# Experts' constants: summed on VectorE and added to X inside the expert slots instead of after them

## What is computed

```python
logits = xf @ wr + br
topk_vals, topk_idx = jax.lax.top_k(logits, K)            # K = 2 of E = 4
gates = jax.nn.softmax(topk_vals, axis=-1)
h = gelu(jnp.einsum('nd,edh->enh', xf, w1) + b1[:, None, :])
y = jnp.einsum('enh,ehd->end', h, w2) + b2[:, None, :]
c = jnp.einsum('eh,ehd->ed', gelu(b1), w2) + b2           # what expert e gives for a zero row
c_sum = c.sum(axis=0)
out = einsum('nk,nkd->nd', gates, y_sel - c_sel + c_sum)  # y_sel, c_sel: rows of the chosen experts
```

## Time and profile before

| | |
|---|---|
| median of 3 runs | 2856.28 us (2854.46 to 2858.55) |
| the profiled execution's own time | 2849.76 us |
| its span, first to last instruction | 2847.9 us |
| mean granted TensorE clock | 0.957 of full speed |
| TensorE busy | 2592.6 us (91%) |
| VectorE busy | 1286.4 us (45%) |
| GpSimd busy | 841.2 us (30%) |
| ScalarE busy | 691.1 us (24%) |

### The profile page before, as it was taken

One profiled execution on the slowest core, in us unless ns is written; L12 is line 12 of the kernel. 1 busy time (PEld: TensorE's weight loads), 2 busy tenths in 40 slices (PEclk: granted clock), 3 DMA queues, 4 the chain that ended last, 5 costly groups with the idle time before them and its releaser, 6 DMA issues.

```text
span 2847.9 us, 29154 instructions
## 1 busy us (share of the span) xinstructions
PE 2592.6 (91%) x10019; PEld 1794.1 (63%) x10019; DVE 1286.4 (45%) x2138; ACT 691.1 (24%) x1127; POOL 841.2 (30%) x794
## 2 busy tenths in 40 slices
PE   5996888978999959999999999999999997966987
PEld 3552333434444448888888888887777676845776
DVE  8785666441111273010010010017888887856554
ACT  2001222121111123121121121124444443123232
POOL 1225665001111055555300000105454451004443
PEclk9998999988999979999999999999999998987999
DMA  4016666163333244232222222226777785447864
GB/s 140 1 38 186 183 180 170 60 227 128 109 118 111 73 156 178 78 107 79 79 100 87 77 80 104 92 77 217 237 230 251 260 250 192 136 177 268 293 236 143
DMA packets 170693, 420.59 MB, mean 148 GB/s; under 512 B 26857, under 2 KB 27657, under 8 KB 170593
## 3 DMA queue, kind: packets, MB, share of 16 engines
q0 software_dynamic: 63008, 191.21, 21.7%
q1 hardware_dynamic: 80320, 178.20, 17.9%
q10 hardware_dynamic: 27264, 49.88, 4.7%
HBM read 332.76 MB, written 92.57 MB: 149 GB/s over the span
## 4 chain that ended last, share of the span: by engine, by line
PE 80%; DVE 7%; DMA 5%; issue 4%; ACT 1%; another core or an unknown queue 1%; POOL 1%; DVEq 1%; SPq 0%; ACTq 0%; POOLq 0%
PE pair L1096 10%; PE pair L1095 10%; PE pair L1094 10%; PE pair L1017 6%; PE pair L1037 6%; PE pair L937 5%; PE pair L879 3%; PE pair L955 2%; PE pair L1118 2%; PE pair L1138 2%; PE pair L1139 2%; PE pair L1140 2%; PE pair L1121 2%; PE pair L919 2%; PE pair L901 2%
## 5 line engine op out<-in xcount | busy, mean ns | idle before, releaser
L1094 PE MATMUL pair<-wh,xh 128*128 128x512 f32 x1200 | 466.8, 389 | 0.0
L1095 PE MATMUL pair<-wh,xl 128*128 128x512 f32 x1200 | 466.8, 389 | 0.0
L1096 PE MATMUL pair<-wl,xh 128*128 128x512 f32 x1200 | 466.8, 389 | 0.0
L1814 DVE TENSOR_TENSOR wl<-raw,wh 128x512 fp32r<-128x512 f32 x136 | 84.0, 689 | 747.1 <-ACT wh L1264 697.7
L794 POOL DMA_INDIRECT rows_y<-y_rows,l_row x184 | 224.1, 1218 | 306.5 <-PE pair L1121 158.6
L1264 ACT ACTIVATE OS<-pair 128x512 f32<-128x512 f32 x170 | 101.8, 599 | 710.2 <-PE pair L1096 596.2
L1095 PEld LDWEIGHTS pair<-wh,xl 128*128 128x128 f32 x1200 | 225.2, 188 | 46.9
L1094 PEld LDWEIGHTS pair<-wh,xh 128*128 128x128 f32 x1200 | 225.2, 188 | 46.8
L1096 PEld LDWEIGHTS pair<-wl,xh 128*128 128x128 f32 x1200 | 225.2, 188 | 46.7
L1264 ACT ACTIVATE high_y<-rows_y,l_inv 128x1024 fp32r<-128x1024 f32 x154 | 177.0, 1154 | 253.1 <-DMA rows_y<-y_rows,l_row 237.8
L1877 DVE SCALAR_TENSOR_TENSOR low_y<-rows_y,l_inv,high_y 128x1024 fp32r<-128x1024 f32 x154 | 197.0, 1284 | 84.8 <-ACT high_y L1264 84.1
(11 more groups left out here) (326 smaller groups left out, 4102.1 us busy)
## 6 DMA issues: line engine op xcount, KB each, us to landing
y_rows<-OS ACTq DMA_DIRECT2D x160, 256.0 KB
raw<-in_L_gnn_weight SPq DMA_DIRECT2D x16, 2048.0 KB
tok_raw<-in_L_ffn_w SPq DMA_DIRECT2D x8, 2048.0 KB
tok_raw<-in_L_ffn_w SPq DMA_DIRECT2D x16, 1024.0 KB, 16.0
exp_bg<-bias_gelu_rows SPq DMA_DIRECT2D x23, 512.0 KB, 4.9
pair<-pair_rows SPq DMA_DIRECT2D x18, 512.0 KB
U<-in_L_ffn_b SPq DMA_DIRECT2D x18, 512.0 KB
exp_w<-in_L_ffn_w SPq DMA_DIRECT2D x4, 2048.0 KB, 13.5
```

The costliest lines, as they stand in the source:

```text
L1094: mm(o, xh[:, m, k, :], wh[:, k, :], start=(k == 0), stop=False)
L1095: mm(o, xl[:, m, k, :], wh[:, k, :], start=False, stop=False)
L1096: last = mm(o, xh[:, m, k, :], wl[:, k, :], start=False, stop=(k == KD - 1))
```

## The change

- The four zero rows are not routed any more; padding rows get a key beyond all experts. `exp_keep` goes, and every slot subtracts gelu(bias). Each expert gets at least one slot (`least=E0`). The number of slots stays 23.
- In slots 11 to 14 VectorE makes the partial sums `c_part[p, :] = sum over k of gelu(b1)[p, k] * w2[k, p, :]`, one expert in each slot, eight instructions of 128x512 each, into the second half of `w`, which expert 0's w1 has left.
- In slot 17 TensorE sums them over the partitions together with b2 into two banks of PSUM that the slots don't use.
- In slots 18 to 22 VectorE adds the sum to X, two tiles in each slot. GpSimd's additions, ScalarE's copy and SP's read of the four rows go.
- SP loads the second half of expert 2 and all of expert 3 in slot 1, after both first gathers have landed, instead of ahead of the slots. The raw weights' load moves from slot 11 to slot 13.
- Four small instructions that made masks go from VectorE's start.

```diff
-ESLOTS = (TOP0 * N_NODES + E0 + E0 * (P - 1)) // P
-ONE_EXPERT = -(-(N_NODES + 1) // P)
+ESLOTS = (TOP0 * N_NODES + E0 * (P - 1)) // P
+ONE_EXPERT = -(-N_NODES // P)
+PARTS_AT, CONST_AT = 11, 17
...
-        c_rows = place("c_rows", "xn", [E0, D])
-        b2_rows = place("b2_rows", "xn", [E0, D], skip=D)
-        csum_rows = place("csum_rows", "b2", [P, D])
+        c_part = place("c_part", "w", [P, D], skip=8 * HALF)
+        b2_rows = place("b2_rows", "w", [E0, D], skip=8 * HALF + D)
...
+        csum_bank = [banks[1], banks[7]]
...
             expert_half(2, 1)
-            sp.wait_ge(v_full, V_ROUTE + len(TOKG))
-            expert_half(2, 0)
-            expert_half(3, 0)
-            expert_half(3, 1)
...
             for s in range(ESLOTS):
+                if s == 1:
+                    sp.wait_ge(v_full, V_ROUTE + len(TOKG))
+                    sp.wait_ge(*exp_rows_here(0))
+                    sp.wait_ge(*exp_rows_here(1))
+                    expert_half(2, 0)
+                    expert_half(3, 0)
+                    expert_half(3, 1)
                 e = sp.value_load(exp_of[0:1, s:s + 1], min_val=0, max_val=E0 - 1)
                 if s >= 1:
                     sp.wait_ge(exp_hm_ready, s)
                 bias_rows(e)
-                if s == ONE_EXPERT + 1:
+                if s == PARTS_AT:
+                    sp.wait_ge(exp_up_full, ONE_EXPERT)
+                    sp.dma_start(b2_rows[:], a["L0_ffn_b2"]).then_inc(b2_in, 16)
+                if s == PARTS_AT + 2:
                     sp.wait_ge(exp_down_full, 2 * ONE_EXPERT)
+                    sp.wait_ge(c_part_ready, 1)
...
-            sp.wait_ge(exp_x_full, 2 * ESLOTS)
-            sp.dma_start(b2_rows[:], a["L0_ffn_b2"]).then_inc(c_in, 16)
             sp.wait_ge(exp_put_done, 16 * ESLOTS)
-            sp.dma_start(c_rows[:], pair_dram[N_NODES:N_NODES + E0, 0, :]).then_inc(c_in, 16)
...
-            pool.wait_ge(csum_kept, 1)
-            for m in range(NT):
-                pool.tensor_tensor(X[:, m, :], X[:, m, :], csum_rows[:], ALU.add).then_inc(csum_added, 1)
...
                 expert_hidden(s)
+                if s == CONST_AT:
+                    pe.wait_ge(c_part_ready, E0)
+                    pe.wait_ge(b2_in, 16)
+                    for h in range(2):
+                        cols = slice(h * HALF, (h + 1) * HALF)
+                        mm(csum_bank[h], ones[:], c_part[:, cols], start=True, stop=False)
+                        mm(csum_bank[h], ones[0:E0, :], b2_rows[:, cols], start=False, stop=True).then_inc(csum_ready, 1)
             expert_down(ESLOTS - 1)
-
-            pe.wait_ge(c_in, 32)
-            pe.wait_ge(v_read, V_LIST0 + 1)
-            for h in range(2):
-                cols = slice(h * HALF, (h + 1) * HALF)
-                o = pairs[3][:, cols]
-                mm(o, ones[0:E0, :], c_rows[:, cols], start=True, stop=False)
-                mm(o, ones[0:E0, :], b2_rows[:, cols], start=False, stop=True).then_inc(csum_ready, 1)
...
-            act.wait_ge(csum_ready, 2)
-            copy(csum_rows[:], pairs[3][:]).then_inc(csum_kept, 1)
...
-            v.tensor_scalar(pad_mask[:, 2:3], iota_part[:], float(SUMROW), None, ALU.is_lt)
+            v.tensor_scalar(pad_mask[:], iota_part[:], float(LAST), None, ALU.is_lt).then_inc(consts_ready, 1)
             v.tensor_scalar(tok_pad[:], tok_id[:], float(N_NODES + 1), 100.0, ALU.is_ge, ALU.mult)
-            link(v.tensor_scalar(pad_mask[:, 1:2], iota_part[:], float(SUMROW), 100.0, ALU.is_ge, ALU.mult))
-            v.tensor_scalar(pad_mask[:, 3:4], iota_part[:], float(SUMROW), None, ALU.subtract)
-            link(v.tensor_scalar(pad_mask[:, 0:1], iota_part[:], float(SUMROW + E0), 100.0, ALU.is_ge, ALU.mult))
-            link(v.tensor_scalar(pad_mask[:, 3:4], pad_mask[:, 3:4], 0.0, pad_mask[:, 0:1], ALU.max, ALU.add))
...
             for k in range(TOP0):
-                v.tensor_copy(pair_key[:, k * NT:(k + 1) * NT - 1], top_f[:, 0:NT - 1, k])
-                past = pad_mask[:, (3, 1)[k]:(3, 1)[k] + 1]
-                last = v.tensor_scalar(pair_key[:, (k + 1) * NT - 1:(k + 1) * NT], top_f[:, NT - 1, k:k + 1], pad_mask[:, 2:3], past, ALU.mult, ALU.add)
+                last = v.tensor_tensor(pair_key[:, k * NT:(k + 1) * NT], top_f[:, :, k], tok_pad[:], ALU.add)
...
+            def constant_part(e):
+
+                dve.wait_ge(exp_up_full, ONE_EXPERT)
+                dve.wait_ge(exp_w_in[e], 48)
+                for k in range(KH):
+                    for h in range(2):
+                        w2 = exp_w[:, E0 - 1 - e, 1, h * KH + k, :]
+                        part = c_part[:, h * HALF:(h + 1) * HALF]
+                        gelu_b = bg_up[:, 1, KH * e + k:KH * e + k + 1]
+                        if e + k == 0:
+                            last = v.tensor_scalar(part, w2, gelu_b, None, ALU.mult)
+                        else:
+                            last = v.scalar_tensor_tensor(part, w2, gelu_b, part, ALU.mult, ALU.add)
+                    if k < KH - 1:
+                        link(last)
+                last.then_inc(c_part_ready, 1)
+                dve.wait_ge(c_part_ready, e + 1)
+
+            def add_constants(tiles):
+
+                dve.wait_ge(csum_ready, 2)
+                for m in tiles:
+                    for h in range(2):
+                        cols = slice(h * HALF, (h + 1) * HALF)
+                        v.tensor_tensor(X[:, m, cols], X[:, m, cols], csum_bank[h], ALU.add).then_inc(csum_read, 1)
...
-                v.scalar_tensor_tensor(exp_h[:], exp_bg[:, 1, :], exp_keep[:, s:s + 1], exp_h[:], ALU.mult, ALU.add).then_inc(exp_hm_ready, 1)
+                v.tensor_tensor(exp_h[:], exp_h[:], exp_bg[:, 1, :], ALU.subtract).then_inc(exp_hm_ready, 1)
                 if s >= 1:
                     keep_out(s - 1)
+                if PARTS_AT <= s < PARTS_AT + E0:
+                    constant_part(s - PARTS_AT)
+                if s > CONST_AT:
+                    add_constants(range(2 * (s - CONST_AT - 1), 2 * (s - CONST_AT)))
...
-                dve.wait_ge(csum_added, m + 1)
+                dve.wait_ge(csum_read, 2 * (m + 1))
```

More of the change, by code:

```diff
@@ L74 @@
 TOKG = [(0, 512), (512, 512), (1024, 256)]
-SUMROW = LAST
-ESLOTS = (TOP0 * N_NODES + E0 + E0 * (P - 1)) // P
-ONE_EXPERT = -(-(N_NODES + 1) // P)
+ESLOTS = (TOP0 * N_NODES + E0 * (P - 1)) // P
+ONE_EXPERT = -(-N_NODES // P)
+PARTS_AT, CONST_AT = 11, 17
 PERMUTED = ET - SCATTERED
@@ L250, in build @@
         bg_rows = place("bg_rows", "sel", [2 * E0 * KH, P])
-        pad_mask = sb("pad_mask", [P, 4])
+        pad_mask = sb("pad_mask", [P, 1])
         eps = sb("eps", [P, 1])
@@ L308, in build @@
         exp_put = sb("exp_put", [P, ESLOTS], I32)
-        exp_keep = sb("exp_keep", [P, ESLOTS])
         exp_of = sb("exp_of", [P, ESLOTS], I32)
@@ L419, in build @@
         exp_down_full, exp_out_ready, exp_put_done, exp_bg_in = map(sem, ("exp_down_full", "exp_out_ready", "exp_put_done", "exp_bg_in"))
-        c_in, csum_kept, csum_added = map(sem, ("c_in", "csum_kept", "csum_added"))
+        b2_in, c_part_ready, csum_read = map(sem, ("b2_in", "c_part_ready", "csum_read"))
         x3_tile_ready, std3_ready, rstd3_ready = map(sem, ("x3_tile_ready", "std3_ready", "rstd3_ready"))
@@ L1070, in _ @@
                 pe.wait_ge(t_read, T_LN3 + 2 * m + 2)
-                if m >= 2:
+                if m < 2:
+                    pe.wait_ge(csum_read, 2 * NT)
+                else:
                     pe.wait_ge(a_read, A_Y + m - 1)
@@ L1740, in _ @@
             dve.wait_ge(v_read, V_DEC + 2 * NT)
-            link(v.tensor_scalar(X[:, NT - 1, :], X[:, NT - 1, :], pad_mask[:, 2:3], None, ALU.mult))
+            link(v.tensor_scalar(X[:, NT - 1, :], X[:, NT - 1, :], pad_mask[:], None, ALU.mult))
             ln_stats(NT - 1).then_inc(stats_ready, 1)
@@ L1775, in gate_values @@
                 link(v.tensor_tensor(gsm[:, 4, :], gsm[:, 3, :], gsm[:, 1, :], ALU.mult))
-            sort(pair_key[:], E0, PT, pair_hot[:], pair_cum[:], pair_pos[:], v_bank[V_PRE0 % 2], V_PRE0, pair_tmp[:], pair_far[:], gate_values)
+            sort(pair_key[:], E0, PT, pair_hot[:], pair_cum[:], pair_pos[:], v_bank[V_PRE0 % 2], V_PRE0, pair_tmp[:], pair_far[:], gate_values, least=E0)
             link(v.tensor_copy(pair_posi[:], pair_pos[:]))
```

2 lines of the change are left out of this document (removed).

## The result

The changed kernel takes **2836.87 us**, the median of four runs (2836.24 to 2838.2). The kernel before took 2855.53 beside it (four runs, 2854.46 to 2858.55). The ratio is 0.9938 with a 95% interval of 0.9926 to 0.9951: 18.7 us or 0.6% faster. The forecast was 2839.7: 16.6 us, added up from the profile of before and taken off the median. Two single runs, 5757 us of the kernel before beside kernels 9 to 12 and 4479 us of kernel 11, are far above all others and are left out of every median and ratio here.

A forecast was written before the change was run, and what follows sets the result against it. TensorE, with 80% of the chain, was taken to bound the kernel. Terms -16.5 + 3.4 + 0.3 - 3.2 - 0.6 = -16.6 us, off the median 2856.28, gave 2839.7 us; range 2834 to 2848.

The forecast's parts named there:

- the main term: After the slots: TensorE's run without holes starts at 1033.6 instead of 1050.11, -16.5 us (bounds -17.5 and -9.3).
- the first gather: Start of the slots: with the weights behind both gathers, the first lands at 646.0, -3.2 us (bounds 0 and -3.4).
- four products in slot 17: Slot 17: four f32 products of 512 columns on TensorE cost 0.86 each, +3.4 us (bounds 3.4 and 3.8).
- constants' parts on VectorE: Slots 11 to 14: 6.1 us of VectorE work in each, under 12.0 of cover, so no cost.
- The tail, first part: After the last scatter: tile 0's pair loads land 6.25 us later, so VectorE starts at 1012.8 (bounds 1011.8 and 1020).
- the rival of a joint landing: After the slots: the eight pair loads finish together at 1020, the tail gives 9.3, total 2847 us; chance 0.11.
- The tail, second part: From VectorE's start on tile 0 to TensorE's hole-free transposes of tile 2: 20.8 us, against 31.0 before.
- The rival of a stretch by GpSimd's issues: Slots 11 to 14: VectorE's constant parts stretch from 6.1 to 15.5 us, costing 14 us, total 2854; chance 0.07.
- The rival that the gather comes no sooner: Start of the slots: the first gather's wait is its own latency, total 2843 us, inside the range; no separate chance given.
- The bias rows of slot 1: Slot 1: they land behind 6.3 MB of weights at about 670, TensorE feels it at 673.9; hidden, 4 us to spare.
- The slower rival: Slot 1: weights at 105 GB/s delay the bias rows to near 712, 21 us net slower, 2878 us; chance 0.04.
- The kernel's start: Start of the kernel: four constant instructions leave VectorE's chain ahead of the edge work, -0.6 us (bounds 0 and -0.7).

The follow-up runs named there:

- kernels 9 to 12: Changed kernel with additions on GpSimd in slots 18 to 22, with three early unread products, with three edits together, and unedited: 2842.62, 2840.71, 2833.70, 2842.65 us.
- kernel 11: Changed kernel with b2 folded into the partial sums and unread TensorE products both after the slots and ahead of the first transposes: 2833.70 us, ratio 0.9926.
- experiment 8: Changed kernel with unread TensorE products, 16 after the last slot and 3 between the transposes of tiles 0 and 1: 2835.27 us, ratio 0.9936.
- Experiment 3: Changed kernel with the additions to X back on GpSimd after the slots, the sum still made in slot 17: 2814.62 us, ratio 1.0003 to the kernel before.
- experiment 7: Changed kernel with b2 added to the partial sums by VectorE in slot 15, leaving one product per half in slot 17: 2836.07 us, ratio 0.9938.
- experiment 1: Changed kernel with the late weights (expert 2's second half, expert 3) loaded ahead of the slots again: 2800.24 us, ratio 0.9950 to the kernel before.
- experiment 5: The changed kernel run again without edits, beside the kernel before: 2839.66 us, ratio 0.9952, 14.8 us faster.
- Experiments 1 and 2: Changed kernel with the late weights early again, 2800.24 us, ratio 0.9950; kernel before with only the late weights moved into slot 1, 2810.35 us, ratio 0.9990.
- Experiment 6: Changed kernel with 4.2 MB of unread copies behind the late weights, ahead of slot 1's bias rows: 2854.9 us, ratio 1.0000 to the kernel before.
- experiment 9: Changed kernel with the additions to X on GpSimd inside slots 18 to 22, two tiles in each: 2842.62 us, ratio 0.9957 to the kernel before.
- experiment 10: Changed kernel with three unread TensorE products ahead of the first transposes of the slots: 2840.71 us, ratio 0.9953 to the kernel before.

## Why the prediction was right, and where it was not

The sum was -16.6 us. The three comparisons of medians gave -18.7, -14.8 and -14.6, their mean -16.0. The part of the sum that G to T2 holds was -16.0, and came out as -14.3. So the mechanism of the main term is right and shown, but that the total came so near is partly luck: the first gather gave 2.2 us less than its term and the products cost 0.8 more, the tail gave 1.0 more, and the medians of the first comparison add 5 us that no term explains. Its terms, predicted and then measured in the profiles of before and after:

| step | predicted | measured |
|---|---|---|
| end of the slots to the hole-free run | -16.5 | -17.5 |
| four products in slot 17 | +3.4 | +4.1 |
| their effect on the first products of slot 18 | 0 | +0.1 |
| additions ahead of wl in slot 22 | +0.3 | 0 to +0.1 |
| the first gather | -3.2 | -1.0 |
| constants' parts on VectorE | 0 | 0 |

**The tail, first part.** I took the pair loads of tile 0 at 6.25 us after the scatter; the first update stands 1016.30 - 1010.50 = 5.80 after it, of which the chain gives the landing 5.29. Tile 0's two loads did not wait for the six behind them, so the rival of a joint landing (T0 at 1020) fell. The Trainium skill, "DMA: Bandwidth & Descriptors", Anatomy of one DMA, gives its rule for DMAs that GpSimd issues, and these are SP's, which the prediction did not say; put to this load it makes 4.4 us. The run lies 1.4 above that and 0.45 below my term.

**The tail, second part.** From the first update to the hole-free transposes I predicted 20.8 us and 20.4 was measured, against 31.0 before. The half clock at the start of the first products was in that number, and experiment 8 shows that it is 2.0 us of it. Experiment 3 shows that both parts of the tail had to go together: with the chain gone and the additions left beside the updates the gain was zero. I had called the old slowness (6.62 us a pair) contention. The page "GPSIMD Engine Reference" of the Trainium skill, Specifications, names contention with VectorE instructions that have two SBUF inputs. The trace of experiment 3 agrees and gives it a size that neither that section nor the earlier trace rows has: VectorE's instruction can wait for the rest of the row of additions, 17.31 us for 1.28.

**The four products.** This term was mis-sized, 3.4 for 4.1. Its price, 0.86 us for 512 f32 columns, holds for the first product and for both in experiment 7. The three that follow a product of another height took 1.05 each, those of 128 partitions like those of 4, and so did the start of slot 18's up products (7.13 us for 7.03). The bounds came from products of one height; the alternation between 128 and 4 partitions was outside their reach. In some executions the clock fell behind them for another 1.7 us, which no row of before shows.

**The constants' parts.** Right. The timeline of the changed kernel in a slot that has one:

```profile
845.37 5.75 DVE L1823 SCALAR_TENSOR_TENSOR c_part<-exp_w,bg_up,c_part 128x512 f32<-128x512 f32 x8
852.16 0.69 DVE L1840 TENSOR_TENSOR exp_h<-pair,exp_bg 128x512 f32<-128x512 f32 x1 [1.04 <-PE pair L1015]
```

5.75 us for a predicted 6.1, in the idle time ahead of the first addition, with 1.04 us left. The rival of a stretch by GpSimd's issues fell. The additions to X took 2.47 us for four, for a predicted 2.8.

**The first gather.** This is the step that failed: "its traffic is over within 655 to 656, some 3.6 us after issue ... With the weights behind both gathers, the first lands at 646.0". It landed at about 648.3, 5.06 us after its issue. Two things were wrong. First, the end of the traffic in a window is not the landing. The profile of experiment 1, with its early weights, gives for all 23 gathers:

```profile
DMA to landing us min/median/max: 4.2/4.5/7.4
```

So a gather that meets a quiet queue lands some 4.2 to 4.5 us after its issue, and the bound of -3.4 was out of reach: 6.99 less 4.5 is 2.5. Second, the first gather is not alone: the second is issued 1.24 us later, and slot 0's bias rows 0.76 us later. That these cost the remaining 0.6 us is argued and was not tried. Over the ten profiles of kernels with late weights and nothing ahead of the transposes, the slots began 4.7 to 5.5 us after the issue, for 6.99 and 6.84 with early weights: a gain of 1.3 to 2.3 us. Of this the profile after kept only 1.0 at slot 1, since TensorE's clock rose no earlier (at 657.4, for 656.6 before) and the first up products took 10.17 us for 9.30. In experiment 5 the clock rose at 650.0 and slot 1 began at 19.3 us for 22.1. Experiments 1 and 2 put the part at 0.7 to 2.0 us in the whole kernel. The rival that the gather comes no sooner, with its -13.4, was about as near as my likeliest case.

**The bias rows of slot 1.** Named, and their margin overstated. I put their landing at 670 and TensorE's demand at 673.9, so 4 us to spare. The timelines of SP and VectorE in the changed kernel:

```profile
651.61 0.99 SPq L520 DMA_DIRECT2D exp_w<-in_L_ffn_w  x2
652.65 8.02 SPq L524 DMA_DIRECT2D exp_w<-in_L_ffn_w  x2
663.75 25.50 SPq L542 DMA_DIRECT2D exp_bg<-bias_gelu_rows  x3
...
675.78 0.69 DVE L1840 TENSOR_TENSOR exp_h<-pair,exp_bg 128x512 f32<-128x512 f32 x1 [12.20 <-DMA exp_bg<-bias_gelu_rows]
```

SP issued the weights at 651.61, not 648, since the second gather landed later, and the bias rows landed at 675.78, 12.0 us after their issue. VectorE stood idle 12.20 us for them. TensorE's transposes, which want the result, came at 679.03 with it ready at 677.85: 1.2 us to spare. The landing is set by the weights ahead, not by its own issue: in the eleven profiles with late weights and nothing more behind them it stands 32.0 to 33.1 us after the first gather, whatever TensorE does meanwhile. So in the seven of them in which the first slot ran faster, TensorE stood idle 0.1 to 0.6 us there, and slot 1 was 0.5 to 1.0 us longer: late weights took back a part of what they gave. I had the landing 27.7 us after the gather. The slower rival (late weights stall slot 1) was thus much nearer than its 0.04 says, by 1 us of landing and not by a halved rate. Experiment 6 shows the mechanism at full size.

**The kernel's start.** The edge work begins at 6.65 us for 7.39, -0.7 for -0.6. At GpSimd's first gather of node rows it is still ahead: 226.0 to 226.6 us in the twelve profiles with the new start, 227.39 and 226.79 in the two with the old one, so by 0.2 to 1.4. Whether it reaches the end the profiles can't say: between there and the slots, executions of one kernel differ by several microseconds.

**What stays open.** Why the profiled pair shows 13.5 us and the medians 18.7. The start of the slots, which differs from execution to execution by more than that difference, was 0.9 later in the profile after, though it was 1.3 ahead at 226. I take the rest for that scatter; but runs without a profile leave no trace, so it was argued and not shown. The new start and the later load of the raw weights were not run by themselves. Nor was it tried what moves the start of the slots, or why the clock falls behind slot 17's products in some executions.

## What to carry to other kernels

Cost work that moves beside a queue of another engine by its place: the same ten additions cost nothing inside the slots on either engine (experiment 9), about 3 us after them on VectorE, and 16 us after them on GpSimd. When loads are moved behind a gather, look at what queues behind them: here the next small load landed 12 us after its issue, and TensorE had 1.2 us to spare, in some executions none. Read a landing from issue to landing and not from where the traffic ends (4.5 us for 3.6 here), and take it as a lower bound where other transfers are issued beside it. Before two executions are compared, look for a place in which one of them lost time by itself: the 1.7 us in slot 17 hid what the late weights are worth.

## What the runs showed of the hardware

- A VectorE instruction with two SBUF inputs can be held for as long as GpSimd keeps adding, where both read SBUF: 17.31 us for 1.28 with seven of ten additions still to come, 5.67 for 0.69 beside two. In the kernel before the two took turns instead: a pair of updates took 6.62 for 2.61, and GpSimd's additions 2.33 to 3.35 us each, where experiment 3 has 2.33 to 2.36. What decides between the two ways was not tried.
- Where f32 products of 4 and of 128 partitions alternate, those that follow the other height took 1.05 us for 0.86 for 512 columns at full clock, whichever of the two heights they had. In four of the ten profiles that have them the granted clock then fell to 0.50, in the one of experiment 5 for some 3 us, with TensorE busy.
- Loads issued one behind the other by SP landed in the order of issue (in the profile after expert 2's half at 661.3, expert 3's last at 674.6, slot 1's bias rows at 675.8). The small one behind 6.3 MB landed 12.0 to 13.9 us after its issue, for a median of 4.9 to 5.2.
- TensorE's clock, once it had risen after three products, fell back to 0.50 when the transposes left gaps (experiment 10); with 19 products in the hole after the slots it stayed at 1.00 to the end of the stretch (experiment 8).
